# A third tile table for layer 0 of a mixture-of-experts and attention kernel, and a new order of stages

## The reference

```python
x = x + 0.5 * ffn(layernorm(x))      # "layer 0" of the text
x = x + attn(layernorm(x))
x = x + 0.5 * ffn(layernorm(x))      # "layer 1" of the text, same weights

def ffn(xf):                          # 8 experts, top 2, d_ff 512
    probs = softmax(xf @ gate_w.T)
    weights, idx = top_k(probs, 2); weights /= weights.sum()
    out_all = (silu(xf @ w1.T) * (xf @ w3.T)) @ w2.T      # per expert
    return sum_k weights[k] * out_all[idx[k]]

def attn(x):                          # per sequence of 512 tokens
    A = 8 largest x[t].x[s] among s < t
    p = softmax(where(A, (x Wq)(x Wk)^T / sqrt(32), -1e9))
    return gelu((mix * x + (1 - mix) * p x) * gain + bias) * scale
```

## Time and profile before

| | us |
|---|---|
| median of 3 runs | 804.46 |
| lowest, highest | 802.52, 806.79 |
| span of the profiled execution | 805.2 |
| PE busy in it | 695.8 |
| DVE busy in it | 561.3 |
| ACT busy in it | 501.8 |
| POOL busy in it | 451.6 |

### The profile page before, as it was taken

The page is one execution under the profiler, slowest core; times in us unless marked ns, Lnnn a source line. Parts: engine busy times, 40 slices in busy tenths (PEclk is TensorE's granted clock), DMA queues, the critical chain, the costliest instruction groups (busy, mean ns, idle before and its releaser), DMA issues.

```text
span 805.2 us, 17412 instructions
## 1 busy us (share of the span) xinstructions
PE 695.8 (86%) x4632; PEld 429.6 (53%) x4632; DVE 561.3 (70%) x1599; ACT 501.8 (62%) x975; POOL 451.6 (56%) x545
## 2 busy tenths in 40 slices
PE   1751458999999999999988999998999889999992
...
DVE  6679782333687887889879898898865624335766
...
PEclk9875689999999999999999999999999999999997
...
GB/s 337 426 221 162 116 211 179 164 134 143 170 206 126 180 159 149 199 160 172 168 171 197 173 192 168 149 186 135 186 158 178 162 201 144 128 164 212 236 246 320
DMA packets 318614, 150.75 MB, mean 187 GB/s; under 512 B 299133, under 2 KB 302589, under 8 KB 317757
## 3 DMA queue, kind: packets, MB, share of 16 engines
...
...
## 4 chain that ended last, share of the span: by engine, by line
PE 48%; DVE 18%; DMA 10%; issue 9%; ACT 6%; SPq 5%; POOL 3%; another core or an unknown queue 1%; POOLq 0%; ACTq 0%; DVEq 0%
PE B L1247 28%; PE B L1263 16%; DVE t_W L1557 2%; DMA yt<-t_W,t_idx 2%; DMA t_ph<-t_p 2%; DMA hs<-t_s,t_POS 2%; POOL hs L960 2%; DMA t_gh<-t_gp 2%; DVE t_s L1614 2%; DVE t_th L1755 1%; DMA t_W<-t_W 1%; PE B L1315 1%; PE B L1276 1%; SPq L1052 1%; DVE t_X L1775 1%
## 5 line engine op out<-in xcount | busy, mean ns | idle before, releaser
L1247 PE MATMUL B<-t_W,t_ht 128*128 x1704 | 398.9, 383 | 22.4 <-DVE t_W L1557 7.1
L1247 PEld LDWEIGHTS B<-t_W,t_ht 128*128 128x128 f16 x1704 | 166.8, 99 | 200.7 <-issue 35.8
L1755 DVE SCALAR_TENSOR_TENSOR t_th<-B,t_K,t_th 128x512 f32<-128x512 f32 x142 | 105.7, 747 | 115.9 <-PE B L1247 90.8
L1008 POOL DMA_INDIRECT yt<-t_W,t_idx x107 | 112.5, 1052 | 119.8 <-ACT t_W L1405 71.8
L1263 PE MATMUL B<-t_W,t_gh 128*128 x1284 | 160.7, 276 | 9.4 <-issue 6.4
L960 POOL DMA_INDIRECT hs<-t_s,t_POS x112 | 116.0, 1035 | 63.0 <-issue 29.0
L1263 PEld LDWEIGHTS B<-t_W,t_gh 128*128 128x128 f16 x1284 | 125.0, 99 | 43.2 <-issue 13.7
L1389 ACT ACTIVATE t_th<-B,t_K 128x512 f32<-128x512 f32 x142 | 96.8, 683 | 76.8 <-PE B L1247 49.1
L1398 ACT ACTIVATE t_gp<-t_th 128x512 f16<-128x512 f32 x107 | 66.2, 624 | 48.3 <-DVE t_th L1755 40.1
L1000 POOL DMA_DIRECT2D t_idx<-hs x142 | 80.1, 569 | 24.0 <-DMA yt<-t_W,t_idx 13.4
L1766 DVE TENSOR_TENSOR t_gp<-t_th,t_gp 128x512 f16<-128x512 f32 x107 | 75.0, 707 | 26.1 <-ACT t_gp L1398 21.3
...
## 6 DMA issues: line engine op xcount, KB each, us to landing
...
t_ht<-hs SPq DMA_TRANSPOSE x142
t_idx<-hs POOLq DMA_DIRECT2D x142, 0.5 KB
...
```

Source lines behind the costliest of these rows:

```text
L1008: eng.indirect_dma_start(yt_d[L], bass.IndirectOffsetOnAxis(ap=IDX[:, n % RING:n % RING + 1], axis=0), YO[n % YR], None).then_inc(d_y[n % ...
L1247: t = eng.matmul(B[b][:], HT[n % HTR][:, (2 * hl + db) * 128:(2 * hl + db) * 128 + 128], W16[:, bass.ds(expert[n] * 4096 + (db * 2048 + wl ...
L1755: eng.scalar_tensor_tensor(out=th[:], in0=B[b1][:], scalar=K[:, 7:8], in1=th[:], op0=ALU.mult, op1=ALU.mult).then_inc(free[b1], 1)
```

## The change

In layer 0 the two parts `(1, 8)` and `(1, 12)` go and a part `(0, 16)` comes, and `KNOWN` gets a table after 16 token tiles. Layer 0 now has three tables: tiles 0 to 8 come from the first, tiles 9 to 24 from the new one, and tiles 25 to 70 from the last. Tiles 9 to 24 are the ones that are full with the first 16 token tiles, so they wait for routers 0 and 1 only. The remainders of the first 16 token tiles stand behind them, and so `last_tile` becomes 38 for batches 0, 1, 2 and 3; from batch 4 on it is what it was. Layer 1 is unchanged. The number of tiles, the work in a tile and in a batch, and the number of transfers for them stay; the new table adds its own instructions on DVE, one set of small matmuls on PE, and one small transfer of its rows' addresses. A table is now at most 56 columns wide, where layer 0's last was 64. `ORDER` is another string; a line of it is shown.

```diff
-PARTS = (((0, 8), (1, 8), (1, 12), (1, 16), (1, 20), (1, 24), (1, 28), (1, 32)),
+PARTS = (((0, 8), (0, 16), (1, 16), (1, 20), (1, 24), (1, 28), (1, 32)),
          ((0, 16), (0, 24), (1, 24), (1, 28), (1, 30), (1, 31), (1, 32)))
-KNOWN = ((8, 32), (16, 24, 32))
+KNOWN = ((8, 16, 32), (16, 24, 32))
...
 ORDER = (
-    "))Bt)%)Bztf%efYeKY())BYY))BttLKL$$KLKL%$$++++qx%wpfeYKvY!!))fDLKL$$++eYYKLKL$++$Bt-^!!%f^!!e++>)q++xwp)Bt^+++++^"
...
+    "))Bt))B%ft))e%zfe(YKYYLKL)$$KYBtLK)%)$+B)L$qt+f++++e%xfYKwep+YYvL!YKL+BD$$KLK-L$t+$++++%qxfwV+e+pY:v+^z=!!!!^!1!"
...
```

More of the change, by code:

```diff
@@ L133 @@
[L133 to L137, removed]
@@ new lines @@
+    ")!1)?++^!+Y=?=?=^!=u?=??==W_>W?:?==+?B=t++??~)=?=?==)?=+%+z??D_!!f^e^;^~_-Y=;$=B!!!$uWtWu?>.?=W~Y;N^;.N=%Sf)P?)>"
+    "!:;V?:._e;>;;>.=$YW;~SW=NB_S?Q$Y?P:~;=>N?;:Q=.?uP~~;~S~~~.QWWWNEt_F>$P$ES%fqxF;;eE>PwpN**.Y;Q;FESv~W~~~N>;~Q:!Y."
+    ";>^NFP:.;SP.E$;NN!!>SS;$QQFPPE*!Wq*F^S;x>wWE.uNSPW;Ppvs3;Q>F;Ws.NS.;!>;;>!N.WQQQDuN*PESF!1W;**-EP;FQE>.[NW!1*WF;"
+    ";W>.^1^1NE~FQ|||*V;;SPSPSQ.N>;;>;QS.EN};FP>S.W*^EFP;;!1Q.>uW;Q*^!1NEh!1N|W*s1;>Wc!!S!hPFQ^EWPF.N*;;>.;!NSPSE^.*Q"
+    "QFS~;E>!PF;E;N_*~.h>PauSPF;NS~EF~.h*QQ;NEFWuW*>;~~~~***.;N>;EFPWS*P.;SMP>EFQQ;EFNS;H*W._yE~>;.NSQF;Wk~y1W>_Q;PPN"
```

46 lines of the change are left out of this document (23 added, 23 removed).

## The result

The changed kernel took 867.46 us (median of 4 runs, 867.15 to 876.47) where the kernel before took 805.62 beside it: 1.082 times as long, 95% interval 1.078 to 1.085. The forecast was 813 us, range 795 to 826. The sign was right; the loss is 62 us, not 9. As ratios the forecast was 1.01 and the end of its range 1.03.

The account below looks back on a forecast made before the run. DVE was taken to set the start, PE the tiles, and DVE the attention once tiles left it. First fetch at 255.5 plus 217 plus a tail of 341.7 gave 814.2, corrected to 813 us, range 795 to 826.

Parts of the forecast that it names:

- what the stretch lasts is 187 plus DVE's idle time: First fetch to tile 71's up: 187 us of DVE work plus 30 us idle, 217 us where it was 252.3.
- The upper bound in my text: First fetch to tile 71: at most 41 us of DVE idle time, if none of the earlier 39.5 us goes.
- The nearest rival, 827 us: Slower by more, 17%: all 39.5 us of DVE idle stay and clock falls add 4.5 us; tile 71 at 486.5.
- From tile 12 to the first fetch: 58 halves of up and 32 down: 117.0 us of PE plus 3.5, so 120.5 us; first fetch at 255.5.
- the step from the first `up` to tile 12: 49.5 us of DVE work beside PE's 40.3, taken as 53 us, bounds 46 and 60, where it took 62.7.
- I carry 341.7 us over: Tile 71's up to the end: same tiles, batches and tables, so 341.7 us as in the kernel before.
- The start: End of scale 1, kept at 54.4 us, to the first up: 26.9 us of DVE work; up at 81.6, was 90.4.
- The two rules weighed: Shared port could delay DVE's split by some us, not counted; PE pauses lower the clock, 1.8 us of PE per fall.
- PE busy under 85% from fetch to tile 71: Sign for the forecast: PE busy under 85% from first fetch to layer 1's first up, which starts after 463.5 us.
- DVE's share: Deciding sign, first fetch to tile 71: at 86% DVE busy the forecast holds, over 90% it is wrong.
- the wait of 10 us at the first L1276: Sign for the forecast: at batch 0's first PE work, PE waits about 10 us for t_hta.
- The sign against the forecast: The forecast would be wrong if layer 1's tail behind 463.5 us were not 342 us long.

Follow-up runs that it names:

- (5): The changed kernel run again without any edit, on another chip: 838.4 against 793.6 us, 1.057 times the kernel before.
- (9): The changed kernel with all 71 layer 0 tiles ahead of the first fetch and the batches in the order of before: 1.182 times the kernel before.
- (8): The changed kernel with all 71 layer 0 tiles ahead of the first fetch, batches in the changed order: 1.198 times the kernel before.
- (6): The changed kernel with the glow of tiles 39 to 70 computing only 64 of its 512 columns: 1.054 times the kernel before.
- (14): The changed kernel with the 8 largest of a row block found three times over in batches 0 to 3: 1.074 times the kernel before.
- (15): The changed kernel with the glow of tiles 39 to 70 computed twice: 1.072 times the kernel before.
- (2): The changed kernel with the order of the kernel before from tile 71's first up on: 1.041 times the kernel before.
- (4): The changed kernel with the order of before from the first up to the first fetch, so routers 2 and 3 stand early: 1.091 times the kernel before.
- the first comparison: The changed kernel measured beside the kernel before, perhaps on a sixth chip: 867.46 against 805.62 us, 1.082 times.

## Why the prediction was wrong

**What held: the direction.** The start became earlier, the first fetch later by more than that, and the attention did not give the difference back. The fetch moved from 211.2 to 273.8 us (forecast 255.5), and tile 71's `up` from 463.5 to 510.6 (forecast 472.5). Every stretch but the first came out longer than forecast: by 9, 16, 20 and 14 us in turn, with 6 less at the start. In (5) the same differences are 3, 6, 18 and 11, with 8 less, so the stretch of the attention leads in both.

**The step that failed most: "what the stretch lasts is 187 plus DVE's idle time", with 30 us of idle.** The page gave 197.1 + 39.7. Two things were off. DVE's work fell by 15.7 us, not by the 25.7 I took off. The list puts 17 tiles' gates less between the fetch and tile 71, but an engine doesn't stand where the list's marks do. In the window there are 15 gates (L1755) and 15 `glow` (L1766) less, 19.1 us, and three more instructions of the residual (L1845), 1.6 us. And the idle time did not shrink by a quarter; nothing of it went. The upper bound in my text (41 us, "nothing goes") was the right value, and I had argued for it myself with the list of waits, before choosing the middle. The nearest rival, 827 us, had this idle time right and was still 40 us short, by the stretches around it. Idle time and work aren't two terms to be added either. Over six runs with the tables of the changed kernel and DVE work between 152.5 and 217.5 us the stretch grows from 220.0 to 246.8:

| DVE busy | stretch | run |
|---|---|---|
| 152.5 | 220.0 | 9 |
| 156.6 | 223.2 | 8 |
| 182.1 | 228.4 | 6 |
| 197.0 | 234.6 | 5 |
| 212.3 | 243.7 | 14 |
| 217.5 | 246.8 | 15 |
| 212.8 | 252.3 | before |

From (9) to (6) the slope is 0.3, from (5) to (14) and (15) 0.6; it never reaches the 1 that my formula has. Each row is one run, and in (8) and (9) the load of PE, ACT and POOL and the clock differ as well, so the slope is no exact figure. In the last row PE is at 241 us. So the 16 tiles that moved ahead of the fetch cost 62.4 us there (117.0 - 54.6) and gave back 15.5 behind it: 3.9 us of price against 1.0 of return for each. That ratio is the answer to where the gain of the early start went.

**From tile 12 to the first fetch: forecast 120.5, measured 136.5.** On the other chips the same instructions took 125.0 to 126.7 in (2), (5) and (6), and 128.0 and 131.3 in (14) and (15). I had the work right (117.0 us of matmuls) and had left no room for what was put among it: routers 2 and 3, whose scatters used to end before tile 12. That is worth 7 to 8 us by (4). The rest, 8 to 10 us, stands in full only in the first comparison. For the step from the first `up` to tile 12 the forecast was 53; measured 61.9, elsewhere 51.4 to 56.2 in (2), (5) and (6). Where it came near, that was luck: I had DVE lead there with 49.5 us of work, and DVE was busy 41.4 us and PE 49.6.

**The tail: "I carry 341.7 us over".** Measured 355.3, elsewhere 347.6 to 354.1, and 344.8 in (8). The same cut with the order of before lasts 334.0 to 338.7 in the runs on the other chips. I had looked at the counts of work behind tile 71 and not at the order, which was searched anew there too. By medians this costs 1.5%.

**The start: forecast 81.6, measured 75.4.** Here I was too careful. The terms behind `scale` 1 were right (26.9 us forecast, 26.0 measured from 49.4 to 75.4 with DVE busy 25.3, blocks of the split still 1.28 us each), but `scale` 1 ended at 49.4 us and not at 54.4. Router 1's choice is done at 39.0 us in the changed kernel and at 48.0 before, so the new order had pulled the whole of DVE's work ahead of `scale` 1 together. I took its start as it was and looked only at what stood behind.

**The two rules weighed.** The split stayed at 1264 to 1299 ns with scatters beside it, so the rows held: nothing was added to the start by the shared port of which the Trainium skill speaks ("SBUF — State Buffer", section "Who interferes with whom"). The clock: with more pauses of PE in the attention the granted clock there was 0.94 of full speed and not 0.99, and PE was busy 715.9 us in all where it was 695.8. In (8), with PE busy 101 of 223 us, it is 0.67. A lower clock is what the Trainium skill ("TensorE: Matmul & The Clock Gate", section "What's actually happening") leads one to expect of a kernel with more pauses. I had given it 4.5 us in one rival and none in the forecast. Some 16 of those 20 us lie in that stretch (193.4 us busy, where the list gave 177.1). How many are on the path no run shows.

**My list of signs.** "PE busy under 85% from fetch to tile 71" came true (193.4 of 236.8, 82%), DVE's share was 83% where I had 86%, and the wait of 10 us at the first L1276 didn't come: PE was busy 13.7 of the 19.2 us ahead of it and stood for short waits. The sign against the forecast that did come is the tail, 355 us where 342 was to hold.
